# Three slots for the edge one-hots of each half group, and two-column clearing matmuls, in a graph kernel's adjacency build

## The reference

```python
src, dst: (20000,) node numbers, sorted by dst; edge_weight: (20000,)
# attention block: edges (and a loop on each node), each edge counted once
out = segment_sum(alpha[:, :, None] * h[src], dst, num_segments=N)
# graph convolution: the same edges with their weights
deg = segment_sum(ew, col, num_segments=n) + 1.0
norm = dinv[row] * ew * dinv[col]
agg = segment_sum(norm[:, None] * x[row], col, num_segments=n)
```

## Time and profile before

| what | value |
|---|---|
| median of 3 runs | 3652.27 us (3647.5 to 3656.41) |
| the profiled execution | 3658.87 us |
| its span, first to last instruction | 3657.2 us |
| PE busy over the span | 2894.7 us (79%) |
| DVE busy over the span | 2098.2 us (57%) |
| stage of the change (first to last matmul) | 17.2 to 336 us |
| mean granted TensorE clock | 0.891 |

### The profile page before, as it was taken

How to read it: one execution, slowest core, us unless ns; L and a number is a source line. 1 busy time by engine, 2 the same in 40 slices (tenths; PEclk the granted TensorE clock), 3 DMA queues, 4 the chain that set the end, 5 groups by cost and what they waited for, 6 DMA issues and landing times. The chain is left out here.

```text
span 3657.2 us, 42656 instructions
## 1 busy us (share of the span) xinstructions
PE 2894.7 (79%) x15884; PEld 2543.7 (70%) x15885; DVE 2098.2 (57%) x2844; ACT 1271.3 (35%) x1928; POOL 291.6 (8%) x232
## 2 busy tenths in 40 slices
PE   6664875984884968978999995987789599799777
PEld 5553675984884958866888883746666477688776
DVE  6654487967967962234434332544289355688754
ACT  1222264744654641111111111003189300566520
POOL 1232040031022000000000000200000000111100
PEclk9988887986996979989999996897999698899988
DMA  0012101110210135200100104012365120434123
GB/s 29 14 28 60 35 35 52 42 46 33 60 46 33 50 89 119 51 14 27 52 26 26 52 26 93 1 42 83 133 136 113 38 92 1 92 83 90 37 69 89
DMA packets 83081, 204.39 MB, mean 56 GB/s; under 512 B 9866, under 2 KB 39164, under 8 KB 81700
## 3 DMA queue, kind: packets, MB, share of 16 engines
q1 hardware_dynamic: 82950, 202.56, 20.7%
HBM read 153.80 MB, written 44.89 MB: 54 GB/s over the span
## 5 line engine op out<-in xcount | busy, mean ns | idle before, releaser
L826 PE MATMUL ps<-h,e_gat_aggregate 125*125 125x193 f32 x2400 | 409.7, 334 | 91.4 <-DVE e_gat_aggregate L810 75.3
L826 PEld LDWEIGHTS ps<-h,e_gat_aggregate 125*125 125x125 f32 x2400 | 403.1, 192 | 98.1 <-DVE e_gat_aggregate L810 79.0
L103 PE MATMUL ps<-w_pair_experts,hidden_experts 128*125 128x384 f32 x1440 | 257.6, 338 | 5.3 <-DVE x L1232 3.5
L103 PE MATMUL ps<-ln_turned,w_pair_experts 128*128 128x512 f32 (+1 forms) x1296 | 251.8, 356 | 9.4 <-DVE w_pair_experts L1216 9.4
L103 PEld LDWEIGHTS ps<-w_pair_experts,hidden_experts 128*125 128x125 f32 x1440 | 250.7, 185 | 10.5 <-DVE x L1232 6.2
L103 PEld LDWEIGHTS ps<-ln_turned,w_pair_experts 128*128 128x128 f32 x1296 | 211.9, 190 | 50.6 <-DVE w_pair_experts L1216 12.2
L103 PE MATMUL ps<-gat_w_pair_gat_scores,x_turned 128*125 128x384 f32 x1080 | 199.6, 348 | 39.7 <-DVE gat_w_pair_gat_scores L684 39.1
L808 DVE TENSOR_TENSOR e_gat_aggregate<-e_gat_aggregate 125x1250 f32<-125x1250 f32 x120 | 175.2, 1460 | 89.9 <-DMA gat_bias_gat_aggregate<-in_gat_b 49.7
L103 PEld LDWEIGHTS ps<-gat_w_pair_gat_scores,x_turned 128*125 128x125 f32 x1080 | 197.9, 193 | 41.2 <-DVE gat_w_pair_gat_scores L684 39.9
L693 DVE SCALAR_TENSOR_TENSOR peak_gat_scores<-far_gat_scores,from_src,peak_gat_scores 125x1250 f32<-125x1250 bf16 x108 | 224.5, 2139 | 1.3 <-ACTq L661 0.2
L314 PE MATMUL ps<-dst_hot_build_adjacency,src_hot_build_adjacency 125*125 125x128 bf16 x2380 | 187.5, 236 | 45.8 <-DVE dst_hot_build_adjacency L267 45.1
(11 more groups left out here) (312 smaller groups left out, 4922.1 us busy)
## 6 DMA issues: line engine op xcount, KB each, us to landing
stock<-in_moe_w SPq DMA_DIRECT2D x16, 1152.0 KB, 6.2
row_gat_aggregate<-r_scratch SPq DMA_DIRECT2D x24, 625.0 KB, 6.7
V_home<-q_scratch SPq DMA_DIRECT2D x48, 312.5 KB, 6.3
rows_dense_rows_from<-node_scratch SPq DMA_DIRECT2D x10, 1080.0 KB
stock<-in_gat_w SPq DMA_DIRECT2D x4, 2304.0 KB, 8.5
q_scratch<-V_home SPq DMA_DIRECT2D x6, 1250.0 KB, 4.5
k_scratch<-V_home SPq DMA_DIRECT2D x6, 1250.0 KB, 4.5
V_home<-k_scratch SPq DMA_DIRECT2D x24, 312.5 KB, 6.2
```

What stands on the lines that cost most here:

```text
L103: last = pe.matmul(out, left(x), right(y), start=start and n == 0, stop=stop and n == 2)
L826: last = pe.matmul(ps[0:TP, bank(head, d // 2), d % 2 * (C + 1):(d % 2 + 1) * (C + 1)], e[:, n % 3, 0, d * TP:(d + 1) * TP], h[:, t, head, :],
```

## The change

Each half gets three slots instead of one. Visit number `base + c` uses slot `visit % 3 * 2 + j`, on DVE and on PE, so the tiles' places now depend on a register in every instruction that writes or reads them. The semaphores are raised at the start so that DVE may run three visits ahead of PE's reads instead of one. The clearing matmuls write two columns of each bank in place of 512, and the tile of zeros shrinks to 125 columns.

```diff
+    DEPTH = 3
...
-    src_hot = ph.sb("src_hot", [TP, 2, N], BF16)
-    dst_hot = ph.sb("dst_hot", [TP, 2, 4, WIN], BF16)
-    zeros = ph.sb("zeros", [TP, BANK], BF16)
+    src_hot = ph.sb("src_hot", [TP, 2 * DEPTH, N], BF16)
+    dst_hot = ph.sb("dst_hot", [TP, 2 * DEPTH, 4, WIN], BF16)
+    zeros = ph.sb("zeros", [TP, TP], BF16)
...
+    def slot(visit, j):
+
+        return bass.ds(visit % DEPTH * 2 + j, 1)
...
-                            v.tensor_scalar(src_hot[:, j, :], nodes[:], edge[:, 1, j, bass.ds(c, 1)], None, ALU.is_equal)
+                            v.tensor_scalar(src_hot[:, slot(base + c, j), :].rearrange("p a n -> p (a n)"), nodes[:], edge[:, 1, j, bass.ds(c, 1)], None, ALU.is_equal)
                             v.scalar_tensor_tensor(
-                                dst_hot[:, j], dests[:, bass.ds(w * WIN, WIN)].unsqueeze(1).broadcast_to([TP, 4, WIN]), edge[:, 0, j, bass.ds(c, 1)],
+                                dst_hot[:, slot(base + c, j)].rearrange("p a k d -> p (a k) d"), dests[:, bass.ds(w * WIN, WIN)].unsqueeze(1).broadcast_to([TP, 4, WIN]), edge[:, 0, j, bass.ds(c, 1)],
...
-            pe.sem_inc(hot_free[0], NP + 1)
-            pe.sem_inc(hot_free[1], NP + 1)
+            pe.sem_inc(hot_free[0], NP + DEPTH)
+            pe.sem_inc(hot_free[1], NP + DEPTH)
...
-                        pe.matmul(ps[0:TP, 3 * odd + b, :], zeros[:, 0:TP], zeros[:], start=True, stop=False,
+                        pe.matmul(ps[0:TP, 3 * odd + b, 0:2], zeros[:], zeros[:, 0:2], start=True, stop=False,
                                   skip_group_check=True)
...
-                                                 src_hot[:, j, t * TP:(t + 1) * TP],
-                                                 dst_hot[:, j].rearrange("p k d -> p (k d)"),
+                                                 src_hot[:, slot(base + c, j), t * TP:(t + 1) * TP].rearrange("p a n -> p (a n)"),
+                                                 dst_hot[:, slot(base + c, j)].rearrange("p a k d -> p (a k d)"),
                                                  start=False, stop=False, skip_group_check=True)
```

## The result

The change makes the kernel slower: 3812.88 us (3808.19 to 3817.65, 4 runs) against 3652.38 (3647.5 to 3656.41, 4 runs). The ratio is 1.0442, with a 95% interval from 1.0427 to 1.0458. The forecast was 3810 us. The profiled execution took 3813.74 us.

A forecast was written before the change was run, and what follows sets the result against it. PE's register instructions were taken to bound the changed stage: 119 visits x 3.56 = 424 us plus 56 us of turns is 480 in place of 319, so 3652 + 158 = 3810 us, range 3725 to 3885.

The forecast's parts named there:

- The forecast case: PE's register instructions bound the edge-matmul stage at 0.10 to 0.165 us a matmul, time 3746 to 3889 us; chance 0.78.
- The step in a half: On PE, one address instruction before each matmul of a visit, with its hand-over: 0.13 us a matmul.
- 1.4 us a turn: PE's time between windows, drain and idle time to the clears and on to the loop head: 56 us for 40.
- the hand-over: Time around a PE register instruction beyond its own, read from gaps in the turns between windows: some 0.07 us.
- The cover: Array and clearing work hides beneath PE's register instructions; even the slower array pace, 0.106 us a matmul, costs only a few us.
- One address for a half: Tile's offset carried in the matmul, so PE's register work is 1.2 us a visit: about 3600 us; chance 0.10.
- Cheaper: PE's address operations partly shared between tiles, 0.06 to 0.10 us a matmul: 3665 to 3745 us; chance 0.07.
- dearer: A register address also slows the matmul's decoding, 0.17 us a matmul or more: over 3890 us; chance 0.05.
- DVE's visit with slots: DVE's address operations for four instructions a visit: about 1.65 us, all beneath PE's 3.56 us.
- The array's 0.069 us a matmul: PE's array time for a whole matmul of this stage, 1.37 us over 20, hidden beneath the register instructions.
- The clears: Narrowing the clearing matmuls before each window was costed at 0; without cover by the longer addresses, -8 us.
- L308 should be near nothing: The clearing matmuls' line, 40.1 us in all before, should show almost no time, with the turns no shorter.

The follow-up runs named there:

- e3: The changed kernel with DVE allowed only one visit ahead instead of three, slots and register addresses kept: 3811.23 us, ratio 1.0430.
- e4w: The changed kernel with register slots for half 0 alone, half 1 at one fixed slot, and clears of 512 columns: 3689.18 us, ratio 1.0098.
- e5w: The changed kernel with register slots for dst_hot alone, src_hot fixed, DVE one visit ahead, clears of 512 columns: 3668.72 us, ratio 1.0045.
- e6w: The kernel before with four fixed slots a half, loop unrolled by two visits, clears of 512 columns: 3587.42 us, ratio 0.9823.
- e1: The kernel before with the two-column clearing matmuls alone, one slot a half at fixed addresses: 3678.76 us, ratio 1.0073.
- e2: The changed kernel with the clears of 512 columns put back, so the three slots alone: 3814.39 us, ratio 1.0445.
- e6: The kernel before with four fixed slots a half, loop unrolled by two visits, two-column clears: 3597.01 us, ratio 0.9852.
- e8: The kernel before with clearing matmuls of 128 columns in place of 512: 3675.22 us, ratio 1.0060.
- e7: The kernel before with two-column clears and three added idle 512-column matmuls a window into an unread bank: 3663.80 us, ratio 1.0025.

## Why the prediction was right

**The mechanism.** The forecast case came true: PE's register instructions bound the stage. The trace has 2499 of them on the matmuls' line, of 46 ns (2400 of about 50 were named), `src_hot` waits for the matmuls for 266.8 us, and the matmuls' own idle time ends with "issue". The experiments tie the loss to them. It stays whole when the lead of DVE is taken away (e3), shrinks with the number of distinct addresses (e4w: 1309 instructions, +31 us of stage; e5w: 238, +12; after: 2499, +158), and turns into a gain of 72 us of stage when the addresses are fixed (e6w).

**The size.** The step in a half was forecast at 0.13 us and is 0.130, though its parts were off by a little each way: 0.050 for the instruction is 0.046, and 0.08 around it is 0.084. From first to last load of a visit 18 x 0.13 + 0.25 = 2.59 us were forecast and 2.55 measured; the rest of the visit, end and head of the loop and the first address, 0.46 + 0.21 + 0.30 = 0.97 against 3.54 - 2.55 = 0.99. The sum of 3.56 us a visit is 3.54, and 1.4 us a turn is 1.37. The stage is 476.0 us where 480 were forecast. So the hand-over read out of PE's turns in the trace of before, 0.07 us, was the number on which the result hung: without it 18 instructions of 46 ns would be 0.83 us in a visit and lie wholly under the array's 1.37. The rule of the Trainium skill (Advanced Engine Details and Errata, section Sequencer and Instruction Queues) that other instructions are read and queued while a register instruction executes gave 0.115 us a step and 32 us less. Here the step is 0.130, 0.015 longer than by that rule. So the trace doesn't bear out that a load and a matmul are passed on for nothing behind a register instruction, but the hand-over is itself known only to 0.01 us (0.063 and 0.073 in the two places), and what else could fill the 0.084 wasn't tested.

**The cover.** All 2380 matmuls after take 327 ns or more, where before's median is 222 and e1's, mostly at the lower level, 314: by these durations the array ran at 1.2 GHz through the whole stage. The stretch's reading of 1.00 doesn't show it, as at the start of the trace of before, where the clock also reads full over the matmuls of the earlier trace rows, 0.106 us each. That it costs nothing was forecast (0.106 us a matmul under 0.13). The run e2 confirms it: the wide clears take its matmuls to the upper level for part of the stage, at a reading of 0.67, and the stage is the same 476 us.

```profile
L319 PE MATMUL ps<-dst_hot_build_adjacency,src_hot_build_adjacency x2380: 220/328/366, 18.6 to 493.0; 125*125 x199
```

**The rivals.** One address for a half, with the tile's offset in the matmul, fell: there is one instruction for each matmul. The time that rival gave, about 3600 us, is near what fixed slots reach (e6), but by another way: the DVE visit of 1.65 us is 1.44 there, since DVE works out no slot either, and 1.92 where it does. With 1.92 the rival's own sum would be 119 x 1.92 + 72 = 300 us of stage, 3633 us and not 3600. "Cheaper" and "dearer" fell with the 0.130.

**What was wrong.** DVE's visit with slots, taken as 1.65 us, is 1.92, which is longer than the 1.83 of before. It didn't matter to the sum, because PE's visit is 3.54, but it means that the lead which the slots give could not have shortened the visits of this kernel even if PE had worked out its addresses for nothing. The array's 0.069 us a matmul spread the gap between the halves over the matmuls; inside a half it is 0.057. This doesn't change the sum either, as the array lies under PE's register instructions.

The clears. They were costed at 0, which e2 confirms for the change. But the sentence "without that cover it would be -8" has the wrong sign: without the cover they cost 21 us of stage and 0.55 to 0.91% of the time (e1). The step took the 0.86 us of three wide matmuls as work to be saved and never asked what they did for the clock of the matmuls that follow. And "L308 should be near nothing" was too low: 19.0 us, 250 ns each in the records, against 40.1 us and 449 ns; three of them take 0.48 us in a turn, so they start (0.48 - 0.25) / 2 = 0.115 us apart. The 25 ns as the least distance, which the prediction names, isn't reached by these matmuls, each with a weight load of its own.

## What to carry to other kernels

An index in a register isn't free because it stands in the operand: count the distinct addresses that an engine must work out in its loop, price each at its instruction and the hand-over around it, and hold the sum against the work beneath, here 0.130 us against 0.057 of matmul (0.106 at the lower clock). Do it for every engine that uses the operand: here DVE's visit went from 1.44 us to 1.92. Where a few buffers rotate, unroll the loop over them, so that every place is fixed and only the loop's own index is in a register. Before shortening or removing matmuls that look idle, look at the granted clock of that stretch; and try two edits of one change apart, since here one hid the other's cost.

## What the runs showed of the hardware that was not expected

- **Wide matmuls that do nothing useful hold TensorE's clock.** 120 clears of 512 columns in 319 us, where the clock is 0.93. With two columns the clock is 0.70 and the stage 21 us longer, with 128 columns 0.70 and 20; with two columns and 120 idle matmuls of 512 it is 0.93 again (e1, e8, e7). The Trainium skill (TensorE: Matmul & The Clock Gate, section HAM oscillation — how this bites in real kernels) describes a kernel whose waits for a DMA between bursts of matmuls send the clock down round after round. The trace of e1 agrees in that the clock falls again and again (0.70 over the stage, 0.50 in the stretch shown), but not in the wait: PE is idle for 339.9 - 252.4 = 88 us of e1's stage and for 318.9 - 220.7 = 98 of before's. What differs is the work in the turn, and e7 shows that work in the turn brings the clock back.
- **A register in the place of `dst_hot` costs a matmul nothing by itself.** With one address for ten matmuls the loads stand (1.32 - 0.14) / 19 = 0.062 us apart, as with fixed places, (1.37 - 0.14) / 19 = 0.065 (e5w; the gap between the halves is in both). For the weights this wasn't tested.
- **A register instruction between two matmuls costs 0.084 us beyond its own 0.046**, which is a little more than the 0.07 between PE's register instructions in a turn. The level of the clock doesn't change it much, if at all: after and e2 both have 476 us of stage.
